# Second pass of a spectral convolution with whitening: two pairs of channels go through TensorE together, two whitenings in a row

## What is computed

```python
# layer 0: x + spectral convolution of the group-normalised x
x = x + _L0_conv_ref(_gn(x), L0_conv_weight_re, L0_conv_weight_im, L0_conv_bias)
#   rfft2, keep 32 x 17 modes, mix the 16 channels of a head by complex weights, irfft2
# layer 1: x + whitening of the group-normalised x
x = x + _L1_conv_ref(_gn(x))
#   covariance over the last axis in groups of 16 columns, Cholesky, inverse, applied to x
```

## Time and profile before

| quantity | value |
|---|---|
| median of three runs | 3468.51 us |
| the profiled execution's own time | 3470.97 us |
| its span, first to last instruction | 3469.1 us |
| mean granted TensorE clock | 0.955 |
| busy share of the span: PE, DVE, ACT, POOL | 84%, 72%, 33%, 32% |
| HBM read and written | 639.40 MB, 361.28 MB |

### The profile page before, as it was taken

The page is one execution under the profiler, slowest core; times in us unless marked ns, Lnnn a source line. Parts: engine busy times, 40 slices in busy tenths (PEclk is TensorE's granted clock), DMA queues, the critical chain, the costliest instruction groups (busy, mean ns, idle before and its releaser), DMA issues.

```text
span 3469.1 us, 230151 instructions
## 1 busy us (share of the span) xinstructions
PE 2899.2 (84%) x98637; PEld 2044.2 (59%) x98637; DVE 2506.5 (72%) x4292; ACT 1131.8 (33%) x2796; POOL 1105.0 (32%) x1460
## 2 busy tenths in 40 slices
PE   6888888888888450665799999999999999999998
PEld 3555555555555450222577777777777777777776
DVE  4777777777777328555577777777777777777777
ACT  1222222222222230000344444444444444444444
POOL 4666666666665105554011111111111111111111
PEclk8999999999999765998799999999999999999999
DMA  7999999999999870997588888888888888888887
GB/s 231 324 327 330 329 324 331 328 322 331 331 329 308 136 101 31 346 355 236 193 300 302 300 302 303 301 301 301 301 301 302 301 301 301 302 300 303 302 300 275
DMA packets 630224, 1001.28 MB, mean 289 GB/s; under 512 B 103712, under 2 KB 464176, under 8 KB 630192
## 3 DMA queue, kind: packets, MB, share of 16 engines
q1 hardware_dynamic: 528816, 912.44, 79.8%
q10 hardware_dynamic: 101376, 88.39, 8.9%
HBM read 639.40 MB, written 361.28 MB: 288 GB/s over the span
## 4 chain that ended last, share of the span: by engine, by line
PE 51%; ACT 14%; issue 13%; ACTq 10%; DMA 7%; DVE 4%; SPq 1%; DVEq 0%; POOL 0%; POOLq 0%
PE bank L598 15%; ACT reg L650 13%; PE bank L589 11%; ACTq L658 6%; PE bank L425 6%; DMA reg<-xh_d 5%; PE bank L436 5%; PE bank L444 4%; PE bank L458 3%; PE bank L569 2%; PE bank L530 1%; PE bank L507 1%; ACT xh L650 1%; DVE reg L870 1%; PE bank L467 1%
## 5 line engine op out<-in xcount | busy, mean ns | idle before, releaser
L650 ACT ACTIVATE reg<-bank 128x512 f32<-128x512 f32 (+2 forms) x1568 | 792.8, 539 | 973.1 <-PE bank L598 945.2
L1063 DVE STREAM_TRANSPOSE reg<-bank 128x256 f32<-128x256 f32 x2048 | 738.8, 418 | 340.0 <-PE bank L615 340.0
L773 POOL TENSOR_TENSOR reg<-reg 128x512 f32<-128x512 f32 x512 | 686.0, 1340 | 431.8 <-PE bank L436 400.7
L1067 DVE SCALAR_TENSOR_TENSOR reg<-reg,m,xht 128x1024 f32<-128x1024 f32 x512 | 657.8, 1285 | 72.1 <-DVE reg L1063 38.2
L598 PE MATMUL bank<-tab,reg 64*128 64x256 f32 x4096 | 695.7, 406 | 0.6 <-DVE reg L1063 0.3
L826 POOL TENSOR_TENSOR reg<-reg,tab 128x64 f32<-128x64 f32 x512 | 165.6, 324 | 1553.3 <-ACT reg L650 827.7
L858 DVE TENSOR_TENSOR reg<-reg 128x512 f32<-128x512 f32 x512 | 529.1, 1034 | 35.4 <-DVE gmask L876 18.9
L615 PE MATMUL bank<-reg 32*32 32x128 f32 x32768 | 548.0, 279 | 1.7 <-DVE reg L1063 1.7
L615 PEld LDWEIGHTS bank<-reg 32*32 32x32 f32 x32768 | 371.9, 103 | 210.3 <-issue 171.7
L589 PE MATMUL bank<-tab,reg 64*128 64x64 f32 x8704 | 444.9, 236 | 45.8 <-ACT reg L650 45.7
L598 PEld LDWEIGHTS bank<-tab,reg 64*128 64x128 f32 x4096 | 460.9, 188 | 28.8 <-issue 1.5
(11 more groups left out here) (126 smaller groups left out, 1759.7 us busy)
## 6 DMA issues: line engine op xcount, KB each, us to landing
reg<-in_x_dram SPq DMA_DIRECT2D x256, 1024.0 KB, 8.4
reg<-in_x_dram SPq DMA_DIRECT2D x512, 512.0 KB, 3.9
out_dram<-reg SPq DMA_DIRECT2D x512, 512.0 KB, 2.9
xh_d<-xh ACTq DMA_DIRECT2D x128, 512.0 KB, 7.1
reg<-xh_d SPq DMA_DIRECT2D x128, 512.0 KB, 5.9
gram_d<-gram ACTq DMA_DIRECT2D x64, 256.0 KB
reg<-gram_d SPq DMA_DIRECT2D x64, 256.0 KB, 4.8
spec_d<-psu ACTq DMA_DIRECT2D x512, 8.5 KB
```

The costliest lines, as they stand in the source:

```text
L650: copy = lambda o, i, **k: nc.scalar.activation(o, i, ACT.Copy, **k)
L773: nc.gpsimd.tensor_tensor(out=halves[:, q % 2, 1], in0=x_in[:, 2 * q:2 * q + 2, 0], in1=x_in[:, 2 * q:2 * q + 2, 1], op=ALU.subtract).then ...
L1063: ins = v.transpose(o_sb[:, q].rearrange("p n (f w) -> p f n w", f=2)[:, :, :, BL * j:BL * j + BL], bank[4 + j][:, 0:W].rearrange("p (f n ...
L1067: v.scalar_tensor_tensor(out=o_sb[:, q], in0=o_sb[:, q], scalar=m1[:, ds(t * 4 + q, 1)], in1=mwhit[:, :].unsqueeze(1).to_broadcast([P, 4, W]),
```

## The change

Two pairs (2m and 2m+1) now form one step, `two(t, m)`, on TensorE, ScalarE and VectorE. In it TensorE turns the next spectrum, widens this one, turns and adds pair 2m (in banks 2 and 3) and pair 2m+1 (in banks 0 and 1, once these hold no spectrum any more), and then whitens pairs 2m-1 and 2m directly after each other, into the right and the left halves of banks 4 to 7. The spectrum is turned by two 64-row products in place of one of 128 rows. `xt_sb` and `wp` have four buffers in place of two. VectorE waits for both whitenings, turns both pairs back and then does both sums. SyncE's loop is unchanged. The core of the diff:

```diff
-        xt_sb, a = cut(big, a, 2, 2, 2, H)
+        xt_sb, a = cut(big, a, 4, 2, 2, H)
-        wp, a = cut(big, a, 2, 2, BL)
+        wp, a = cut(big, a, 4, 2, BL)
...
+            def spectrum_turned(t, m, first=False):
                 pe.wait_ge(*nth("cs_ready", t * 2 + m + 1))
-                pe.wait_ge(*nth("z_ready", t * 2 + m))
-                mm(bank[0][:, W:W + P], cs[:, m].rearrange("p a b -> p (a b)"), T("eye"), start=True, stop=True,
-                   is_transpose=True).then_inc(S["ct_mm"], 1)
+                if not first:
+                    pe.wait_ge(*nth("xt2_copied", t * 8 + 4 * m - 4))
+                    pe.wait_ge(*nth("ct_ready", t * 2 + m))
+                for c in range(2):
+                    k = slice(KH * c, KH * c + KH)
+                    ins = mm(bank[c][:, W:W + KH], cs[k, m].rearrange("p a b -> p (a b)"), T("eye")[k, k],
+                             start=True, stop=True, is_transpose=c == 1)
+                ins.then_inc(S["ct_mm"], 1)
...
+            def turn(t, q, last=False, first=False):
+                m, e = q // 2, q % 2
                 pe.wait_ge(*nth(f"x_re_in{q}", t * 16 + 16))
-                pe.wait_ge(*nth("xt2_copied", t * 8 + 2 * q))
+                if e == 0:
+                    pe.wait_ge(*nth("xt2_copied", t * 8 + 4 * m))
+                else:
+                    pe.wait_ge(*nth("ct_ready", t * 2 + m + (1 if last else 2)))
...
+                if e == 0:
+                    pe.wait_ge(*nth("z_ready", t * 2 + m + 1))
                 for half in range(2):
                     for c in range(2):
...
-                        if half == 1 and c == 1 and before is not None:
-                            may_whiten(*before)
+                        if e == half == c == 1:
+                            may_whiten(t, m)
...
+            def may_whiten(t, m):
+                pe.wait_ge(*nth("w_ready", t * 4 + 2 * m + 1))
+                pe.wait_ge(*nth("xt2_copied", t * 8 + 4 * m + 2))
+                pe.wait_ge(*nth("o_turned", t * 4 + 2 * m - 1))
...
+            def two(t, m, last=False, first=False):
+                if not last:
+                    spectrum_turned(*((t, 1) if m == 0 else (t + 1, 0)))
+                widened(t, m)
+                turn(t, 2 * m)
+                turn(t, 2 * m + 1, last)
+                if not first:
+                    whitened(2 * m - 1 if m else 3)
+                whitened(2 * m)
...
+            def two(t, m, last=False):            # ScalarE
+                widened_kept(t, m)
+                if not last:
+                    turned_kept(*((t, 1) if m == 0 else (t + 1, 0)))
+                for e in range(2):
+                    q = 2 * m + e
+                    act.wait_ge(*nth("o_mm", t * 4 + q - 3))
                     for c in range(2):
                         act.wait_ge(*nth("xt2_mm", t * 8 + 2 * q + c + 1))
-                        copy(xt_sb[:, q % 2, :, c], bank[2 + c][:, :].rearrange("p (f h) -> p f h", f=2)
+                        copy(xt_sb[:, q, :, c], bank[2 - 2 * e + c][:, :].rearrange("p (f h) -> p f h", f=2)
                              ).then_inc(S["xt2_copied"], 1)
+                if not last:
+                    for e in range(2):
+                        scaled(*((t, 2 + e) if m == 0 else (t + 1, e)))
...
+            def two(t, m, first=False):           # VectorE
+                former = (t, 1) if m else (t - 1, 3)
+                dve.wait_ge(*nth("o_mm", t * 4 + 2 * m + 1))
+                for which in (turned_back, result):
+                    if not first:
+                        which(*former)
+                    which(t, 2 * m)
```

More of the change, by code:

```diff
@@ L619, in whitened @@
                 ins.then_inc(S["o_mm"], 1)
[L621 to L636, removed]
-            with pe.Fori(1, NP // 4 - 1) as t:
[L638 to L641, removed]
+            def two(t, m, last=False, first=False):
[7 more added lines that the diff above has]
+                whitened(2 * m)
+            spectrum_turned(0, 0, first=True)
+            two(0, 0, first=True)
+            two(0, 1)
+            with pe.Fori(1, NP // 4 - 1) as t:
+                two(t, 0)
+                two(t, 1)
+            two(NP // 4 - 1, 0)
+            two(NP // 4 - 1, 1, last=True)
+            pe.wait_ge(*nth("w_ready", NP))
+            pe.wait_ge(*nth("xt2_copied", NP * 2))
+            pe.wait_ge(*nth("o_turned", NP - 1))
+            whitened(3)
         def root(act, n, a):
@@ L817, in four @@
                 for q in range(4):
[L818 to L821, removed]
                     e = q % 2
                     pool.wait_ge(*nth("w_scaled", t * 4 + q + 1))
-                    pool.wait_ge(*nth("o_mm", t * 4 + q - 1))
-                    nc.gpsimd.tensor_tensor(out=wp[:, e], in0=wr[:, e],
+                    pool.wait_ge(*nth("o_mm", t * 4 + q - 3))
+                    nc.gpsimd.tensor_tensor(out=wp[:, q], in0=wr[:, e],
                                             in1=T("eye32").rearrange("p (a b) -> p a b", a=2),
                                             op=ALU.add).then_inc(S["w_ready"], 1)
+                    if e == 1 and not last:
+                        spectrum_of(t + 1, q // 2)
             spectrum_of(0, 0)
+            spectrum_of(0, 1)
             with pool.Fori(0, NP // 4 - 1) as t:
@@ L1058, in _, with turned_back @@
             dve.wait_ge(*nth("mw_ready", 1))
-            def result(t, q):
-                dve.wait_ge(*nth(f"out_stored{q}", t * 16))
-                dve.wait_ge(*nth("o_mm", t * 4 + q + 1))
-                for j in range(4):
-                    ins = v.transpose(o_sb[:, q].rearrange("p n (f w) -> p f n w", f=2)[:, :, :, BL * j:BL * j + BL],
-                                      bank[4 + j][:, 0:W].rearrange("p (f n h) -> p f n h", f=2, n=4))
-                ins.then_inc(S["o_turned"], 1)
+            def turned_back(t, q):
+                dve.wait_ge(*nth(f"out_stored{q}", t * 16))
+                for j in range(4):
+                    at = W * (q % 2)
+                    ins = v.transpose(o_sb[:, q].rearrange("p n (f w) -> p f n w", f=2)[:, :, :, BL * j:BL * j + BL],
+                                      bank[4 + j][:, at:at + W].rearrange("p (f n h) -> p f n h", f=2, n=4))
+                ins.then_inc(S["o_turned"], 1)
+            def result(t, q):
                 dve.wait_ge(*nth("o_turned", t * 4 + q + 1))
@@ L1069, in result @@
                                        op0=ALU.add, op1=ALU.subtract).then_inc(S["o_ready"], 1)
-            def four(t, first=False):
-                for q in range(4):
-                    if q >= 1:
-                        result(t, q - 1)
-                    elif not first:
-                        result(t - 1, 3)
-            four(0, first=True)
-            with dve.Fori(1, NP // 4 - 1) as t:
-                four(t)
-            four(NP // 4 - 1)
+            def two(t, m, first=False):
[5 more added lines that the diff above has]
+                    which(t, 2 * m)
+            two(0, 0, first=True)
+            two(0, 1)
+            with dve.Fori(1, NP // 4) as t:
+                two(t, 0)
+                two(t, 1)
+            dve.wait_ge(*nth("o_mm", NP))
+            turned_back(NP // 4 - 1, 3)
             result(NP // 4 - 1, 3)
```

39 lines of the change are left out of this document (13 added, 26 removed).

## The result

The changed kernel takes 3770.97 us (3767.42 to 3778.47, 4 runs); the kernel before took 3468.05 beside it. The ratio is 1.087, 95% interval 1.0853 to 1.0887: 303 us slower. The forecast was 3620 with a range of 3490 to 3700. The direction was right, the size was half of what came, and the range did not hold it.

A forecast was written before the change was run, and what follows sets the result against it. The TensorE-ScalarE handover of banks 2 and 3 was taken to bound the kernel at 6.95 us a step; late loads would make it 7.55, so 256 steps add 154 us to 3470.97, written as 3620 us, range 3490 to 3700.

The forecast's parts named there:

- What bounds the kernel before: Second pass: TensorE and ScalarE hand banks 2 and 3 back and forth; a two-pair step takes 6.95 us.
- TensorE's own work: TensorE's two-pair step without waits: 5.7 us, with 0.54 more for a second whitening directly behind the first.
- The handover's floor: TensorE and ScalarE, from one whitening to the next, with ScalarE's copies between: 6.1 us a step.
- Loads that hang on the sums: SyncE's loads, issued behind stores and so behind VectorE's sums, come late: 7.55 us a step, +154 us.
- the chain: From a whitening's start through sum, stores and second load to the second next whitening: 15.14 us for two steps.
- the four transfers: Two stores and two loads in a row in one queue: 1.45 + 5.93 us, all landed at 13.38.
- The clock: Rival, 4%: TensorE's clock falls in the long steps, adding 0.65 us a step, giving 3790 us.
- Loads in time: Rival, 12%: the second load lands early enough, the 6.1 us handover binds, 3250 us and up to 3320.
- only the first load counts: Rival, 6%: the second load overtakes or shares engines with the second store; 7.0 us a step, about 3480.
- the rows' price: DMA cost read from the profile's rows: 1.45 us fixed plus 1.48 us for each 512 KB transfer.
- The count of changes of tile shape: TensorE: six tiling-mode changes a step become two, each draining TensorE by the skill's rule.
- The signs named ahead: Profile: TensorE's DMA waits 2 to 3 us per two steps, paired whitenings, alternating spacing, DMA share 0.79 and 278 GB/s.

The follow-up runs named there:

- Loads ahead: Kernel before, with SyncE's loop reordered so each step issues both loads before the two stores: 3474.24 us, ratio 0.9997.
- the moved wait: Kernel before, with the wait ahead of each whitening moved behind the last addition and the widening, carried by a one-column product: 3471.69 us, ratio 0.9995.
- the 64-row turn: Kernel before, with the spectrum turned by two 64-row products in place of one of 128 rows: 3464.12 us, ratio 0.9979.
- experiment 1: Changed kernel, with SyncE's loop reordered so both loads are issued ahead of the two stores: 3376.98 us, ratio to the kernel before 0.9732.
- experiment 3: Changed kernel with filler products nobody reads ahead of the waits for loads: 3713.52 us with two and two, 3685.64 us with two and four.
- the fastest version: Changed kernel with loads issued ahead of stores and the wait ahead of the whitenings moved behind the last addition: 3309.62 us, ratio to before 0.9534.

## Why the prediction was right and wrong

*What bounds the kernel before: right.* Loads ahead, the moved wait and the 64-row turn change it by 0, 0 and 8 us (experiments 2, 8, 6). That leaves the handover with ScalarE; no run made ScalarE itself faster.

*TensorE's own work: mostly right.* The second whitening in a row took 1.90 - 1.07 = 0.83 us more, not 0.54. I had taken the stream of the first pass as the nearer row, but its records have 32 columns and those of the whitening 128; the 0.80 of the weight loads, kept as a bound, was near the value. VectorE's transposes start at 1.94 for 1.64.

*The handover's floor: right within 0.4.* I worked out 6.1; short steps took 6.46 and loads ahead 6.58, with the 0.29 of the second whitening in it.

*Loads that hang on the sums: right.* SyncE's program was the cause, by experiment 1, and the chain agrees nearly term by term: 6.05 for 6.00, 7.90 for 7.83, 13.76 for 13.42, 15.48 for 15.14. Its own cost is 7.72 to 7.79 (the full-clock stretches and experiment 3) - 6.95 = 0.77 to 0.84 a step, 197 to 215 us, for a forecast of 154. The term that was low is the four transfers: 13.76 - 6.05 = 7.71 from the first store to the data of the second load, for 1.45 + 5.93 + 0.04 = 7.42, so 0.29 of the 0.34 in two steps; over the 75 full-clock stretches it is 0.20 of 0.30. The longer whitening did not lengthen the chain: 8 transposes took 2.77 and a sum 1.22, for 2.90 and 1.29, and the first store left 0.05 late.

*The clock: wrong, and this is the step that failed.* The sum of 7.55 a step put the lower clock at nothing; I had it as a rival of 4% beside the forecast, "it would add 1.3 to the tail of the chain, 0.65 a step: 3790". It belongs into the forecast: late loads make the waits, and with the waits came the lower clock, in 18% of the time. The remaining 8.16 - 7.72 to 7.79 = 0.37 to 0.44 a step, 95 to 113 us, is that; experiment 3 shows 85 us of it directly. With the chain alone at 7.72 the time would have been some 3665 us, inside the range. That the rival's 3790 lies near the measured 3771 is partly luck: its chain was 0.17 a step too short and its clock term, 0.65, 0.2 to 0.3 too high. My evidence against it, the middle part with PE busy 65% at clock 1.00, compared busy shares. In that part of the kernel before each wait is short, 1.1 us at most:

```profile
1491.98 1.20 PE L530 MATMUL bank<-reg 128*64 128x290 f32 x8 [1.08 <-DMA reg<-xh_d]
1493.38 1.20 PE L530 MATMUL bank<-reg 128*64 128x290 f32 x8 [0.20 <-DMA reg<-xh_d]
```

In the changed kernel PE was busy 85% by its records, the clock still fell, and with fillers in the waits it mostly did not. But the waits alone do not settle it either: between 1700 and 3700 us TensorE had 99 of more than 1.5 us, and after a part of them, as in the two steps shown, the clock stayed at 1.00; so it did with PE busy 85% from 2560 to 2580 us. Which length or which share decides I can't say from these runs.

*The rivals.* Loads in time (12%) is what experiment 1 makes by hand, 3377; unaided it did not occur. That only the first load counts fell: TensorE waits on both. The estimate by the figures of the Trainium skill, "DMA: Bandwidth & Descriptors", "Anatomy of one DMA" (2.0 us and 436 GB/s, for another issuing path), made two steps 14.6; at the full clock they were 15.4, so the rows' price was nearer, and itself too low. The count of changes of tile shape in the rival of the loads in time was one too high before: five become two where the 34-row products count as tiles of 64 rows.

*The signs named ahead.* Waits for DMA on the transposes, whitenings in twos (128 records in 1.90, not 1.6), alternate steps of 6.5 and 9.0 and VectorE's longer wait all came (742 us over 245 steps, 3.0, for a forecast of 1.9, by the longer steps). The waits were not "on odd pairs above all": they are 204 us on the first pair of a step and 52 on the second, since in the long step TensorE comes to the first load first and stands there; the second is still the one whose data come last, 1.72 before the whitening. Loads landed after 4.4 and 5.7 us in turn (medians), for 3.9 and 5.5. DMA's share of 0.79 and the 278 GB/s were nearly met in the third experiment at the full clock (0.77 and 269), not in the changed kernel (0.74, 257).

## What to carry to other kernels

When several units of work are bunched, look at the queue whose program isn't in the diff: a load written behind a store inherits every delay of the result it stores, and doubling the unit both delays the result and brings forward the use. Issue loads on the freeing of their buffer alone. And treat the clock as a consequence, not as a rival: where a forecast contains new waits of TensorE, price the sum at both levels.

A wait that guards the next phase can be put behind the last work of this one, not on it: here that was worth 67 us, and nothing where another engine was the bound.

## What the runs showed of the hardware that was not expected

The clock fell to 0.50 with TensorE busy 85% of the stretch, and four to six additional products a step, some 0.66 us for two of them, kept it at 0.99 to 1.00 and made the kernel faster although its work grew. A second batch of 64 records of 32 x 32 products directly behind the first took 0.83 us more, although a stream of as many records of 32 columns in the first pass took some 0.54 without its tail; being in a row saved only 0.24 us of 1.07. The 0.33 us of "issue" ahead of the whitening's weight loads went when a product of one column stood between, though the change of tile shape stayed. And 512 KB transfers kept some 350 GB/s of pace in bunches and in even flow alike: 257 GB/s at a share of 0.74 in the changed kernel is 347, and 332 GB/s at a share of 0.93 in the fastest version, with no wait for a load, is 357.
